# Attention gates folded into the output weights, LayerNorm statistics taken behind each addition, and three of four blocks normalised by ScalarE

## The reference, cut to what matters

```
ga = (2*(ga >= 0) - 1) * maximum(abs(ga), 0.25)      # gate of the attention, one row per batch
h = layernorm(x) * (1 + ca) + sa
x = x + ga * attention(h)                            # ends in  o @ Wo
h = layernorm(x) * (1 + cb) + sb
x = x + gb * feed_forward(h)
layernorm(x) = (x - mean) / sqrt(var + 1e-5)         # over the 128 features of a token
```

## Time and profile before

| | |
|---|---|
| median of 3 executions | 3150.76 us (3150.07 to 3151.40) |
| the profiled execution, its own time | 3150.11 us |
| its span, first to last instruction | 3148.3 us |
| TensorE matmul busy | 2853.6 us (91%) |
| VectorE busy | 2314.3 us (74%) |
| ScalarE busy | 1970.9 us (63%) |
| GpSimd busy | 1226.9 us (39%) |
| granted TensorE clock, mean | 0.927 of full speed |

### The profile page before, as it was taken

One profiled execution on the slowest core, in us unless ns is written; L12 is line 12 of the kernel. 1 busy time (PEld: TensorE's weight loads), 2 busy tenths in 40 slices (PEclk: granted clock), 3 DMA queues, 4 the chain that ended last, 5 costly groups with the idle time before them and its releaser, 6 DMA issues.

```text
span 3148.3 us, 88094 instructions
## 1 busy us (share of the span) xinstructions
PE 2853.6 (91%) x36283; PEld 1716.4 (55%) x36340; DVE 2314.3 (74%) x4012; ACT 1970.9 (63%) x5637; POOL 1226.9 (39%) x911
## 2 busy tenths in 40 slices
PE   5689888778898899999599999999999999999997
PEld 4444577523345233333366666666666666666664
DVE  5740487289703777776688888888888888888885
ACT  4532464174222466666388888877888878888785
POOL 0110012000000111110377766776766676676662
PEclk7589955889899799999799999999999999999999
DMA  2000000000000200000322323233222332322222
GB/s 108 3 1 1 38 4 3 1 0 0 1 0 19 59 24 23 23 22 10 123 69 67 81 69 90 67 81 102 67 70 69 102 81 61 97 69 67 65 60 51
DMA packets 48239, 153.40 MB, mean 49 GB/s; under 512 B 11552, under 2 KB 13856, under 8 KB 45952
## 3 DMA queue, kind: packets, MB, share of 16 engines
q1 hardware_dynamic: 47872, 148.17, 17.9%
HBM read 43.60 MB, written 5.44 MB: 16 GB/s over the span
## 4 chain that ended last, share of the span: by engine, by line
PE 70%; DVE 16%; ACT 8%; issue 3%; DVEq 2%; DMA 1%; ACTq 0%; POOLq 0%; POOL 0%; SPq 0%
PE ps L1627 14%; PE ps L756 7%; PE ps L1645 5%; PE ps L1680 5%; DVE arena L1127 4%; PE ps L1222 4%; PE ps L1250 4%; PE ps L1689 4%; PE ps L1702 4%; PE ps L1237 3%; PE ps L1662 3%; PE ps L1671 3%; PE ps L1708 2%; DVE arena L2095 1%; PE ps L1654 1%
## 5 line engine op out<-in xcount | busy, mean ns | idle before, releaser
L1627 PE MATMUL ps<-arena 128*128 128x512 f32 x1152 | 563.3, 611 | 16.8 <-ACTq L1914 16.4
L1979 ACT ACTIVATE arena<-ps,arena 128x64 f32<-128x64 f32 x1536 | 458.8, 318 | 86.1 <-DVE arena L2175 82.5
L2252 POOL TENSOR_TENSOR arena<-arena 128x1024 f32<-128x1024 f32 x190 | 447.4, 2360 | 97.8 <-DVE arena L2064 97.8
L2258 POOL TENSOR_TENSOR arena<-arena 128x2048 f32<-128x2048 f32 x95 | 344.3, 3624 | 225.1 <-ACT arena L1921 220.2
L1387 DVE TENSOR_REDUCE arena<-ps 128x1 f32<-128x512 f32 x512 | 329.5, 686 | 76.8 <-PE ps L1222 71.7
L1349 ACT ACTIVATE arena<-ps 128x1024 f32<-128x1024 f32 x256 | 262.2, 1024 | 178.3 <-PE ps L1237 169.6
L1979 ACT ACTIVATION_READ_ACCUMULATOR arena<-ps,arena 128x1 f32 x1536 | 323.3, 211 | 0.0
L1627 PEld LDWEIGHTS ps<-arena 128*128 128x128 f32 x1152 | 197.5, 191 | 182.4 <-issue 157.7
L191 POOL TENSOR_SCALAR rstd<-mv 128x4 f32<-128x4 f32 x32 | 8.1, 252 | 681.6 <-DVE mv L178 681.6
L2059 DVE TENSOR_TENSOR arena<-ps,arena 128x1024 f32<-128x1024 f32 x192 | 234.2, 1220 | 47.0 <-PE ps L1627 32.7
L2064 DVE TENSOR_TENSOR arena<-ps,arena 128x512 f32<-128x512 f32 x384 | 245.6, 682 | 0.0
(11 more groups left out here) (286 smaller groups left out, 5532.4 us busy)
## 6 DMA issues: line engine op xcount, KB each, us to landing
arena<-pack_l SPq DMA_DIRECT2D x144, 256.0 KB
arena<-grow SPq DMA_DIRECT2D x144, 256.0 KB
arena<-in_deep SPq DMA_DIRECT2D x6, 2649.5 KB, 11.0
arena<-pack_l SPq DMA_DIRECT2D x96, 128.0 KB
arena<-grow SPq DMA_DIRECT2D x84, 128.0 KB
arena<-in_rotary SPq DMA_DIRECT2D x6, 1024.0 KB, 7.4
pack_tern<-in_tern SPq DMA_DIRECT2D x2, 2888.0 KB, 10.2
arena<-scr_q SPq DMA_DIRECT2D x96, 48.0 KB
```

Of the source, the lines that this page charges most:

```text
L1627: last = T.matmul(m.ps[0:rows.stop - rows.start, at + half, :], f.xs[t % 2][:, rows], w.wqkv[:, j * INNER + half * BLK:j * INNER + (half + ...
L1979: last = A(f.prob[:, p, :], m.ps[:, 4 + j % 2, i * SPAN:(i + 1) * SPAN], ACT.Exp, bias=f.nmax[t % 2][:, p:p + 1], accum_out=f.rsum[t % 2][ ...
L2252: G.tensor_tensor(f.rot[t % 2][:, here], f.rot[t % 2][:, here], f.sin[:, here], ALU.add)
L2258: G.tensor_tensor(r, r, spread(f.ss[t % 2], DH), ALU.mult).then_inc(s["rotated"], 1)
```

## The change

Three things are changed together.

- **Gates in the output weights.** The attention's output matrix is multiplied by the gate row once per batch (`gated_weights`, two VectorE operations per layer, of 128 or 256 columns), and the last product of the attention uses `wog` instead of `wo`. Behind it `add_block` is one addition of a bank to x. The feed-forward stages keep `add_gated`.
- **Statistics behind each addition.** `ln_block` stands in the loops of the stage before: as soon as a block of x is complete, VectorE takes its statistics. The barriers between an attention or a feed-forward stage and the LayerNorm behind it are gone; 10 stages are left of 17.
- **Normalisation by ScalarE.** GpSimd makes -mean * rstd as well, with two more operations. ScalarE normalises blocks 0 to 2 with four activations each; block 3 is normalised by VectorE as before. `LN_BANKS` says into which banks each LayerNorm transposes.

```
-def ln_vector(nc, dve, m, s, k):
-    for g in range(NBLK):
-        tiles = range(4 * g, 4 * g + 4)
+def ln_block(nc, dve, m, s, k, g):
+    tiles = range(4 * g, 4 * g + 4)
+    dve.drain()
+    for t in tiles:
+        nc.vector.bn_stats(m.stats[:, t, :], m.x[:, t, :])
+    dve.drain()
+    for t in tiles:
+        last = nc.vector.bn_aggr(m.mv[:, t, :], m.stats[:, t, :])
+    last.then_inc(s["stats"], 1)
+    if g == NBLK - 1:
+        dve.wait_ge(s["rstd"], NBLK * (k + 1))
         for t in tiles:
-            nc.vector.bn_stats(m.stats[:, t, :], m.x[:, t, :])
-        dve.drain()
-        for t in tiles:
-            last = nc.vector.bn_aggr(m.mv[:, t, :], m.stats[:, t, :])
-        last.then_inc(s["stats"], 1)
-    for t in range(TILES):
-        if t % 4 == 0:
-            dve.wait_ge(s["rstd"], NBLK * k + t // 4 + 1)
-        nc.vector.tensor_scalar(m.xn[:, t, :], m.x[:, t, :], m.mv[:, t, 0:1], m.rstd[:, t:t + 1],
-                                ALU.subtract, ALU.mult).then_inc(s["xn"], 1)
+            last = nc.vector.tensor_scalar(m.xn[:, t, :], m.x[:, t, :], m.mv[:, t, 0:1], m.rstd[:, t:t + 1],
+                                           ALU.subtract, ALU.mult)
+        last.then_inc(s["xn_last"], 1)
...
-        nc.gpsimd.tensor_tensor(m.rstd[:, here], m.rstd[:, here], m.nhalf[:, 0:4], ALU.pow).then_inc(s["rstd"], 1)
+        root = nc.gpsimd.tensor_tensor(m.rstd[:, here], m.rstd[:, here], m.nhalf[:, 0:4], ALU.pow)
+        if g == NBLK - 1:
+            root.then_inc(s["rstd"], 1)
+            continue
+        nc.gpsimd.tensor_scalar(m.shift[:, here], m.mv[:, here, 0], -1.0, None, ALU.mult)
+        pool.drain()
+        nc.gpsimd.tensor_tensor(m.shift[:, here], m.shift[:, here], m.rstd[:, here], ALU.mult).then_inc(s["rstd"], 1)
...
+LN_BANKS = (0, 4, 0, 4, 0, 0, 0, 4)
...
 def ln_scalar(nc, act, m, s, k, l, sub):
-    for g in range(NBLK):
+    def normed(g):
+        act.wait_ge(s["rstd"], NBLK * k + g + 1)
+        for t in range(4 * g, 4 * g + 4):
+            last = nc.scalar.activation(m.xn[:, t, :], m.x[:, t, :], ACT.Identity, bias=m.shift[:, t:t + 1],
+                                        scale=m.rstd[:, t:t + 1])
+        last.then_inc(s["xn"], 1)
+
+    def modulated(g):
         b = g // (NBLK // BATCH)
         act.wait_ge(s["turned"], NBLK * k + g + 1)
...
+    normed(0)
+    normed(1)
+    modulated(0)
+    normed(2)
+    for g in range(1, NBLK):
+        modulated(g)
+
+def gated_weights(nc, dve, m, l, wog, wo, blocks):
+    dve.wait_ge(m.loaded["l%d" % l], 16)
+    for b in range(BATCH):
+        nc.vector.tensor_tensor(wog[:, b, :, :], wo, repeat(gate_row(m, l, ATTN, b), blocks), ALU.mult)
+
+def add_block(nc, m, ps, i):
+    x = m.x[:, 4 * i:4 * i + 4, :]
+    nc.vector.tensor_tensor(x, ps.rearrange("p (a b) -> p a b", a=4), x, ALU.add)
...
     V.memset(g.at[:, :, :, :], 0.0)
+    gated_weights(nc, dve, m, g.layer, g.wog, g.wo, g.vd // P)
...
     for i in range(NBLK):
         dve.wait_ge(s["y"], i + 1)
-        add_gated(...)
+        add_block(nc, m, m.ps[:, 4 + i, :], i)
+        ln_block(nc, dve, m, ln, 2 * g.layer + 1, i)
```

More of the change, by code:

```diff
@@ L196, in ln_tensor @@
+LN_BANKS = (0, 4, 0, 4, 0, 0, 0, 4)
 def ln_tensor(nc, pe, m, s, k):
     for g in range(NBLK):
-        pe.wait_ge(s["xn"], TILES * k + 4 * (g + 1))
+        if g < NBLK - 1:
+            pe.wait_ge(s["xn"], (NBLK - 1) * k + g + 1)
+        else:
+            pe.wait_ge(s["xn_last"], k + 1)
         for t in range(4):
-            last = nc.tensor.transpose(m.ps[:, g, t * P:(t + 1) * P], m.xn[:, 4 * g + t, :], m.ident)
+            last = nc.tensor.transpose(m.ps[:, LN_BANKS[k] + g, t * P:(t + 1) * P], m.xn[:, 4 * g + t, :], m.ident)
@@ L201, in ln_tensor @@
         last.then_inc(s["turned"], 1)
 def ln_scalar(nc, act, m, s, k, l, sub):
-    for g in range(NBLK):
+    def normed(g):
[5 more added lines that the diff above has]
+    def modulated(g):
         b = g // (NBLK // BATCH)
         act.wait_ge(s["turned"], NBLK * k + g + 1)
-        nc.scalar.activation(m.hT[:, g * BLK:(g + 1) * BLK], m.ps[:, g, :], ACT.Identity,
+        nc.scalar.activation(m.hT[:, g * BLK:(g + 1) * BLK], m.ps[:, LN_BANKS[k] + g, :], ACT.Identity,
@@ L212 @@
 MOD_SEMS = ("silu", "cols", "wide", "rows")
-LN_SEMS = ("stats", "rstd", "xn", "turned")
+LN_SEMS = ("stats", "rstd", "xn", "xn_last", "turned")
 def add_gated(nc, dve, m, ps, t0, n, row, tmp):
@@ L368, in projected @@
                 last = T.matmul(m.ps[:, 4 + i, t * P:(t + 1) * P], g.oT[:, k, (4 * i + t) * P:(4 * i + t + 1) * P],
-                                g.wo[:, k, :], start=k == 0, stop=k == blocks - 1)
+                                g.wog[:, i // (NBLK // BATCH), k, :], start=k == 0, stop=k == blocks - 1)
         last.then_inc(s["y"], 1)
@@ L807, in tern_vector @@
                   repeat(f.row[:, i // 2, :], 4), f.tmp[:, i % 2, :].rearrange("p (a b) -> p a b", a=4))
+        ln_block(nc, dve, m, ln, 2 * f.layer + 2, i)
 TERN_SEMS = {"up": 16, "silu": 16, "glu": 16, "hid": 32, "hid_read": 32, "y": 4}
@@ L965, in mole_vector @@
                   f.tmp[:, bank % 2, 0:n * P].rearrange("p (a b) -> p a b", a=n))
+        if bank % 3:
+            ln_block(nc, dve, m, ln, 4, 2 * (bank // 3) + bank % 3 - 1)
 MOLE_SEMS = ("low", "gated", "turned", "zT", "hid", "hidden", "logits", "exped", "y")
@@ L1008, in projected @@
     def projected(j, t):
[L1010 removed]
+        return T.matmul(m.ps[:, t // 4, (t % 4) * P:(t % 4 + 1) * P], f.y[:, j, t * P:(t + 1) * P],
+                        f.wog[:, t // BT, j, :],
                         start=j == 0 and t % 4 == 0, stop=j == INB - 1, skip_group_check=True)
@@ L1151, in ssm_setup @@
     f.arate = a.take(INB * STATES)
-    f.tmp = f.decay[:, 0, 0:2 * BLK].rearrange("p (a b) -> p a b", a=2)
+    f.wog = a.take(BATCH * INB * P).rearrange("p (b k n) -> p b k n", b=BATCH, n=P)
     return f
@@ L1298, in mha_tensor @@
         for t in range(BT):
-            last = T.matmul(m.ps[:, 4 + 2 * b + t // 4, (t % 4) * P:(t % 4 + 1) * P], f.oT[b][:, t * P:(t + 1) * P], f.wo,
+            last = T.matmul(m.ps[:, 4 + 2 * b + t // 4, (t % 4) * P:(t % 4 + 1) * P], f.oT[b][:, t * P:(t + 1) * P], f.wog[:, b, 0, :],
                             start=True, stop=True)
@@ L1557, in mha_setup @@
     f.all = a.take(PAIRS * BT * WIDTH)
+    f.wog = a.take(BATCH * P).rearrange("p (b k n) -> p b k n", b=BATCH, n=P)
     f.prob = a.take(BT * SEQ).rearrange("p (a b) -> p a b", a=BT)
@@ L1565, in mha_setup @@
     f.oT = [late.take(SEQ) for _ in range(BATCH)]
-    f.tmp = late.take(2 * BLK).rearrange("p (a b) -> p a b", a=2)
     return f
```

73 lines of the change are left out of this document (34 added, 39 removed).

## The result

| | before | after |
|---|---|---|
| median | 3150.41 us (4 executions, the first three among them; 3148.96 to 3151.4) | 3134.03 us (4 executions, 3132.21 to 3135.03) |
| ratio to before, 95% | | 0.9946 [0.9934, 0.9959] |
| profiled execution, its own time | 3150.11 us | 3132.21 us |
| its span | 3148.3 us | 3130.4 us |
| granted TensorE clock, mean | 0.927 | 0.928 |

The change is a gain of 16.4 us, 0.54%. The forecast was 26.6 us and 3124.2. The direction was right; the time lies at the upper end of the last range given (3117 to 3134), outside the range that the forecast gave itself by small errors (3119 to 3130), and 10 us of the gain are missing.

The account below looks back on a forecast made before the run. Bound: the wait chain at eight LayerNorms, along VectorE, then TensorE's transposes and ScalarE. 28.2 us saved less 1.6 paid gives -26.6, from profiled 3150.11 to 3123.5; median 0.65 higher, 3124.2. Small-error range 3119 to 3130, final range 3117 to 3134.

Parts of the forecast that it names:

- The bound and the order: LayerNorms 1 to 7: statistics and normalising of early blocks overlap the stage before, saving 28.2 us together.
- ScalarE's activation: ScalarE normalising blocks 0 to 2: 0.31 us per 128x128 activation, four per block 1.24 us.
- LayerNorm 0: First LayerNorm, x complete from the start: GpSimd's pace decides, block 3 normalised from 37.6, costing 1.2 us.
- The gates' cost in the softmax attention: Head of the softmax attention, VectorE on the chain: two gate operations at 0.21 us cost 0.4 us.
- the clock as a small swing: TensorE's clock at stage heads: 6 us gained or lost, 3118 or 3130; none taken in the sum.
- the prediction's own signs of being wrong, the last one: Stage heads: a TensorE clock of 0.5 for longer than 4 us would show the prediction wrong.
- GpSimd becomes the pace: Rival, LayerNorms: GpSimd's multiply costs as much as a power, 2.82 us per block, 11 us back, 3135; chance 0.10.
- The clock in the long stage: Rival, six blocks of layer 3: granted clock falls from 0.99 to 0.96, some 49 us more, 3173; slower, chance 0.03.
- No gain: Rival, all LayerNorms: ScalarE waits for late GpSimd signals, so nothing overlaps and time stays 3150; chance 0.02.
- The clock at the head of a stage: Rival, three stage heads: full clock earlier gives 3118, low clock longer 3130; both extremes together chance 0.04.

Follow-up runs that it names:

- e3: Kernel before with only the gates folded into the output weights, no new order: 3140.27 us, ratio 0.997.
- e2: Kernel after plus many matmuls on constants, read by nothing, ahead of TensorE's wait for each block: 3146.76 us, ratio 0.9988.
- e5: e6 plus matmuls that nothing reads, in counts sized to TensorE's pauses, and one behind the last transposes: 3119.82 us, ratio 0.9909.
- e9: e5 with seven added matmuls in LayerNorm 0 instead of 15, no drain ahead of its first statistics, -mean issued earlier: 3117.29 us, ratio 0.9895.
- e10: Kernel before plus nine added matmuls (seven in LayerNorm 0) ahead of each LayerNorm's transposes and one behind: 3147.01 us, ratio 0.9989.
- e6: Kernel after with LayerNorm 0 normalised by VectorE and without GpSimd's shift there: 3129.06 us, ratio 0.9934.

## Why the prediction was right in its direction and short in its size

- **The bound and the order: right.** The LayerNorms 1 to 7 were forecast to save 3.8, 5.05, 5.2, 1.0, 4.0, 5.05 and 4.1; they saved 3.54, 5.12, 4.88, 0.59, 3.66, 5.13 and 3.77. The sum is 26.7 of 28.2. The mixture came out as reasoned: its last statistics start 10.7 us behind its first multiply (forecast 10.3).
- **ScalarE's activation: mis-sized.** The nearest row, 0.31, was another activation; this one, with two pointers, is recorded at 0.48. Four in a row start 0.39 apart and take 1.65 (in the timeline of LayerNorm 1 above), 0.41 each. GpSimd's two new operations were near their prices; these are their groups in the kernel after, busy time and mean ns of one behind the bar:

```profile
L202 POOL TENSOR_TENSOR shift<-shift,rstd 128x4 f32<-128x4 f32 x24 | 4.8, 200 | 3.8 <-issue 0.4
L200 POOL TENSOR_SCALAR shift<-mv 128x4 f32<-128x4 f32 x24 | 8.4, 348 | 1.6
```

The multiply takes 0.20, near the 0.25 taken and far from the 1.04 of the rival; the -mean takes 0.24 in most places and 0.62 to 0.70 in the ternary stages, while VectorE adds 512 columns, where it is hidden.

The Trainium skill, "ScalarE: Activation LUTs", Rules for kernel authors, gave about 0.41 for an activation with a pointer bias. The trace agrees for the average of a block's four, not for the single record of 0.48; by it the sum was -25.7.

- **LayerNorm 0: nearly right, in part by luck.** Block 3 is normalised from 37.58, where 37.6 was forecast, because two errors cancel: GpSimd began at 29.68 instead of 30.08, and it took up a block every 2.15 instead of 2.03. By its own length it costs 1.77, because its first statistics also begin 0.33 earlier; the next stage starts at 40.76 in place of 39.32, 1.44 later, of 1.2 forecast.
- **The gates' cost in the softmax attention: not seen.** The two operations take 0.49 there, as priced (0.4):

```profile
1001.36 0.49 DVE L246 TENSOR_TENSOR arena<-pack_l,grow 128x128 f32<-128x128 f32 x2
```

but the stage took 480.35 with the gates alone (e3), 481.67 without and 482.9 in the change: it moves more from other causes.

- **The step that failed: the insides of the stages taken as unchanged, with the clock as a small swing.** I gave the swings +6 and -6 at three heads, leaned to the gain because the pauses shrink, and took none in the sum. Against it: +7.3 us inside the stages, 4.2 of it at one head that I had not looked at, the mixture; rows 12 were of a ternary head and the long stage. The longest pause did shrink (ahead of LayerNorm 5's transposes from 10.69 us to 4.75), but TensorE's transposes, which had been one run of 3.7 to 4.1 us, became groups with pauses between, and half clock lasted longer at four heads: 5.42 and 5.93 for 3.70 in the first eight matmuls behind LayerNorms 0 and 6, 7.03 for 5.38 in the mixture's products, 5.95 for 3.61 in the matmuls behind LayerNorm 2 (which cost nothing: that scan stage is 0.66 shorter inside). e2, e5 and e9 show that filling the pauses takes this back, e10 against e9 that nothing else is in it for the four stages of that table. That the grouping is what keeps the clock low fits the table of three heads but is not shown alone. In the prediction's own signs of being wrong, the last one came true: in the mixture the clock was at 0.50 from 536 to 556 us, far longer than 4. With the pauses filled in both, the change is worth 3147.01 - 3117.29 = 29.7 us by the medians, 26.9 by the spans; without the 1.2 us of e9's mended LayerNorm 0 that is 28.5 and 25.7, with the sum of 26.6 between them. Of the spans' 8.7 us that are missing from 26.6, the insides hold 7.3 and the LayerNorms 1.5.

The Trainium skill, "TensorE: Matmul & The Clock Gate", HAM oscillation, warns of breaks between bursts of matmuls. The profile of the change agrees in kind (0.50 through 20 us of work with pauses of 0.7 to 3.5 us in it); I had cited it and leaned to the gain.

- **The rivals.** "GpSimd becomes the pace" named 3135 us, within a microsecond of the measurement, by a multiply of over 1 us that took 0.20: the number was right by chance and the mechanism absent. "The clock in the long stage" did not occur: 0.99 over the last 1630 us before and after. "No gain" is excluded by the timelines. "The clock at the head of a stage" was the right mechanism, leaned the wrong way and priced too low: it named 3130 at worst.

What stays open: why half clock lasts longer behind grouped transposes; why e6 and the kernel after, with the same code around the mixture, differ by 3.1 us there; and the 1 to 3 us by which the two scan stages, the softmax attention and the last stage move from kernel to kernel, which also hide where e10 lost a part of its gain.

## What to carry to other kernels

Work that is spread out to overlap better also spreads out TensorE's small jobs, and what the engine does before a stage can change the clock at which it starts it (filling its pauses did so here at nearly every head): price the first microseconds of every following stage at both clocks, and look at each head, not at one. If the pauses can't be closed, a few matmuls that nobody reads, sized by their measured duration to end before the next real one is due, can be worth more than they cost (9.2 us in e5, 2.6 in e10); too many cost all of it (e2). And judge the parts of a change with the pauses filled, or by more executions: without that, the medians here gave ScalarE's share a sign that lay within their spread.

## What the runs showed of the hardware that was not expected

- A float32 matmul of 384 columns is recorded as two, 0.33 us each at full clock (16 records in 5.3 us for 8 in e2). In LayerNorm 0 of e5 the 15 took 12.96 us, 0.86 each, begun at half clock (0.50 from 28 to 32 us).
- More work made the kernel faster: e5 adds 70 matmuls to e6, 15 of them in LayerNorm 0, and is 9.2 us faster.
- The granted clock is repeatable in places and not in others: the mixture took 70.06 in both profiles of the kernel after, and the ternary stages 143.04 or 143.05 in every kernel whose pauses were filled, but the mixture took 66.92 in e6 with the same code.
- The scan stage of layer 1 runs at half clock from 400 to 520 us, though TensorE is recorded busy for 110 of these 120 us; the window in the kernel after:

```profile
400.00:520.00 120.00, 110.31 (x3216) 88.46 (x3216) 101.47 (x246) 72.55 (x265) 19.48 (x30) 0.50 0.01 4
```

In the kernel before the same window has 0.50 too. Nothing tried here shortens this stage by more than 0.7 us, and why it stays at 0.50 was not looked into.
